# A fused transformer kernel on one core: the GELU up projection as three float32r products of split operands

## The reference, cut to what matters

```python
sa = _mha(x, x, None, sq_w, sq_b, ...)
x = _self_output(sa, x, so_w, so_b, so_g, so_be)          # project, residual, layer norm
inter = jax.nn.gelu(x @ fi_w + fi_b, approximate=False)   # 2048 x 256 by 256 x 1024
x = _self_output(inter, x, fo_w, fo_b, fo_g, fo_be)       # 2048 x 1024 by 1024 x 256
```

## Time and profile before

| | us |
|---|---|
| median of 3 runs (1096.51 to 1098.58) | 1096.81 |
| span of the profiled execution (first to last instruction) | 1094.8 |
| PE busy | 1019.2 (93%) |
| DVE busy | 782.0 (71%) |
| ACT busy | 607.7 (56%) |
| POOL busy | 331.8 (30%) |
| mean granted TensorE clock | 0.975 |

### The profile page before, as it was taken

The page is one execution under the profiler, slowest core; times in us unless marked ns, Lnnn a source line. Parts: engine busy times, 40 slices in busy tenths (PEclk is TensorE's granted clock), DMA queues, the critical chain, the costliest instruction groups (busy, mean ns, idle before and its releaser), DMA issues.

```text
span 1094.8 us, 20748 instructions
## 1 busy us (share of the span) xinstructions
PE 1019.2 (93%) x7648; PEld 601.0 (55%) x7648; DVE 782.0 (71%) x1337; ACT 607.7 (56%) x1191; POOL 331.8 (30%) x724
## 2 busy tenths in 40 slices
PE   5999989999999999999988898989898999999998
PEld 3675666433333333333344665648677676576865
DVE  4786577689999999999723747546536756887565
ACT  2665554478888888888853123131222456556543
POOL 3422111001010343344103334373366433530000
PEclk9999999889999999999998997999999999999999
DMA  7302221451221212212125100021344301100000
GB/s 213 70 16 88 87 68 66 144 188 44 75 71 48 70 49 69 79 45 70 47 67 191 34 15 10 20 77 44 101 155 132 100 31 49 44 25 1 16 18 26
DMA packets 97578, 75.67 MB, mean 69 GB/s; under 512 B 49806, under 2 KB 87483, under 8 KB 97223
## 3 DMA queue, kind: packets, MB, share of 16 engines
q1 hardware_dynamic: 94407, 65.95, 20.0%
q0 software_dynamic: 3072, 8.39, 2.4%
HBM read 42.94 MB, written 30.93 MB: 67 GB/s over the span
## 4 chain that ended last, share of the span: by engine, by line
PE 65%; DVE 10%; DMA 8%; issue 5%; POOL 4%; ACT 4%; SPq 3%; POOLq 0%; DVEq 0%; ACTq 0%
PE OUT L855 15%; PE TR L855 14%; PE OUT L1090 9%; PE TR L861 8%; PE TR L1079 7%; DMA head_q<-MT 7%; PE OUT L1079 3%; PE TR L931 3%; PE SCR L915 2%; POOL dispatched L2038 2%; SPq L697 2%; ACT PTS L1298 2%; PE SCR L908 2%; DVE small L1486 1%; PE OUT L861 1%
## 5 line engine op out<-in xcount | busy, mean ns | idle before, releaser
L1555 DVE TENSOR_REDUCE small<-SCR 128x1 f32<-128x1024 f32 x256 | 308.5, 1223 | 26.2 <-PE SCR L962 20.3
L1396 ACT ACTIVATE shared<-TR 128x512 f32<-128x512 f32 x352 | 200.1, 597 | 38.8 <-PE TR L1079 30.7
L962 PE MATMUL SCR<-head_k,head_q 48*128 48x512 f32 x512 | 193.9, 456 | 2.7 <-DVE P L1531 2.7
L1090 PE MATMUL OUT<-shared,HM 128*32 128x256 f32 x2048 | 165.3, 394 | 1.2 <-ACT shared L1396 0.4
L1079 PE MATMUL TR<-head_q,head_k 51*128 51x512 f32 x352 | 149.7, 463 | 0.9 <-issue 0.6
L1919 POOL TENSOR_SCALAR small<-small 128x1 f32<-128x1 f32 x112 | 27.7, 247 | 346.7 <-DVE small L1487 344.5
L855 PE MATMUL TR<-xT,fifo 128*128 128x512 f32 x224 | 105.8, 629 | 1.1 <-ACT xT L1276 1.0
L1396 ACT ACTIVATE shared<-OUT 128x512 f32<-128x512 f32 x160 | 95.8, 599 | 19.3 <-PE OUT L1079 17.6
L1079 PEld LDWEIGHTS TR<-head_q,head_k 51*128 51x128 f32 x352 | 60.6, 186 | 76.4 <-ACT shared L1396 56.5
L1276 ACT ACTIVATE xT<-TR 128x256 f32<-128x256 f32 x96 | 35.4, 381 | 111.5 <-PE TR L861 108.6
L1090 PEld LDWEIGHTS OUT<-shared,HM 128*32 128x32 f32 x2048 | 41.4, 108 | 93.1 <-ACT shared L1396 57.6
(11 more groups left out here) (241 smaller groups left out, 1860.3 us busy)
## 6 DMA issues: line engine op xcount, KB each, us to landing
pieces<-pieces SPq DMA_DIRECT2D x16, 512.0 KB, 2.7
HM<-dispatched SPq DMA_DIRECT2D x46, 128.0 KB
expert_out<-HM SPq DMA_DIRECT2D x46, 128.0 KB
dispatched<-HB SPq DMA_DIRECT2D x6, 768.0 KB, 4.0
head_q<-pieces SPq DMA_DIRECT2D x32, 128.0 KB
head_k<-pieces SPq DMA_DIRECT2D x32, 128.0 KB
shared<-in_L_ffn_w SPq DMA_DIRECT2D x4, 1024.0 KB, 12.0
x<-TOK SPq DMA_DIRECT2D x16, 128.0 KB, 1.7
```

Source lines behind the costliest of these rows:

```text
L962: ins = nc.tensor.matmul(SQ[kt % 2][:, hf, :], QX[n % 2][rows, kt * 128:(kt + 1) * 128], KX[n % 2][rows, hf * 512:(hf + 1) * 512], start=T ...
L1090: ins = nc.tensor.matmul(PV[32 * g:32 * g + 32, 0:256], VH[:, n % 2, kt, :], PTB[:, kt % 2, g * 256:(g + 1) * 256], start=(kt == 0), stop= ...
L1396: nc.scalar.activation(PTB[:, kt % 2, hf * 512:(hf + 1) * 512], ring_bank("t_scores", n, kt, hf), ACT.Exp, scale=DH ** -0.5).then_inc(st_d ...
L1555: nc.vector.tensor_reduce(nm[:, n % 2, kt:kt + 1], SQ[kt % 2].rearrange("p h n -> p (h n)"), AX, ALU.max, negate=True).then_inc(sq_done.se ...
```

## The change

`fi` is split in two float32r parts, high (`FIH`, in the place of `P`) and low (`FIL`, in the place of `fi` itself), by GpSimd in heads 1 to 8: a cast and a subtraction of 256 columns in each. The transposed input is split as well: `LX.t` now transposes into a bank of OUT, ScalarE copies the bank as float32r into `XGH`, and VectorE subtracts `XGH` from the bank into `XGL` and gives the bank back. `FI.k` has six float32r products for each m (high by high, high by low, low by high, for both halves of the features) instead of two float32 products. As `P` is used for the parts, its last columns are zeroed again by a new step `PZ` (one memset of VectorE) late in the experts. In the diff `gelu_input` stands three times, in TensorE's, ScalarE's and VectorE's stream in this order. The table of steps is otherwise unchanged.

```diff
-    "LX": dict(tr=1),
+    "LX": dict(out=1, xhi=1),
+    "PZ": dict(),
...
-HT.34 QP.0 DM.5 CG.7 RX.5 XL.37 DN.34 UP.36 YS.33 XL.38 S.0 XT.37 HT.35 XT.38 UP.37 XL.39 L3.5 HT.36 E.0 CB.4 UP.38
+HT.34 PZ QP.0 DM.5 CG.7 RX.5 XL.37 DN.34 UP.36 YS.33 XL.38 S.0 XT.37 HT.35 XT.38 UP.37 XL.39 L3.5 HT.36 E.0 CB.4 UP.38
...
+        FIH = over("gelu_up_high", [128, KD, F], F32R, "P")
+        FIL = over("gelu_up_low", [128, KD, F], F32R, "fifo")
+        XGH = over("gelu_in_high", [128, KD, N], F32R, "xT3")
+        XGL = over("gelu_in_low", [128, KD, N], F32R, "P", KD * F)
...
+                def gelu_input(t):
+                    pe.wait_ge(tok_ready.sem, tl.after(tok_ready, "SN", t))
+                    bank = out_bank(tl)
+                    transposes(bank, [XN[:, t % BT, k * 128:(k + 1) * 128] for k in range(KD)]).then_inc(out_full.sem, 1)
+
                 def gelu_up(k):
-                    at.block_copied("LX", k)
+                    pe.wait_ge(out_done.sem, tl.after_block(out_done, "LX", k))
+                    pe.wait_ge(fi_ready, 1)
                     for m in range(MF):
-                        at.feature_major(fi, xTb, m)
+                        c = slice(m * 128, (m + 1) * 128)
+                        bank = tr_bank(tl)
+                        product(bank, [(w[:, f, c], x[:, f, :]) for f in range(KD)
+                                       for w, x in ((FIH, XGH), (FIH, XGL), (FIL, XGH))]).then_inc(tr_full.sem, 1)
...
+                def gelu_input(t):
+                    bank = OUT[:, tl.slot(out_full, 2), :]
+                    act.wait_ge(out_full.sem, tl.next(out_full))
+                    c = t % BT * 128
+                    nc.scalar.activation(XGH[:, :, c:c + 128], bank[:, 0:256].rearrange("p (k n) -> p k n", k=KD), ACT.Copy)\
+                        .then_inc(xg_ready.sem, 1)
...
+                def gelu_input(t):
+
+                    bank = filled(tl)
+                    dve.wait_ge(xg_ready.sem, tl.next(xg_ready))
+                    c = t % BT * 128
+                    signal_out(tl, nc.vector.tensor_tensor(
+                        XGL[:, :, c:c + 128], bank[:, 0:256].rearrange("p (k n) -> p k n", k=KD),
+                        XGH[:, :, c:c + 128].bitcast(F32), ALU.subtract))
+
+                def key_columns():
+
+                    dve.wait_ge(tr_full.sem, tl.after(tr_full, "FI", T // BT - 1))
+                    nc.vector.memset(P[:, :, :, SC1:KP], 0.0)
...
             for n in range(NH):
+                if n == 1:
+                    pool.wait_ge(d_fifo, 16 * 2)
+                if 1 <= n < 1 + 4 * KD:
+                    k, c = divmod(n - 1, 4)
+                    part = (slice(None), k, slice(c * 256, (c + 1) * 256))
+                    chain(nc.gpsimd.tensor_copy(FIH[part], fi[part]))
+                    ins = nc.gpsimd.tensor_tensor(FIL[part], fi[part], FIH[part].bitcast(F32), ALU.subtract)
+                    if n == 4 * KD:
+                        ins.then_inc(fi_ready, 1)
...
-                pool.wait_ge(tr_done.sem, tl.after(tr_done, "LX", t))
+                pool.wait_ge(out_full.sem, tl.after(out_full, "LX", t))
                 add_bias(XN[:, t % BT, :], "fo_b")
```

More of the change, by code:

```diff
@@ L272, in schedule_c @@
             before((a, i - 2), (b, i))
+    before(("PZ",), ("S", 0))
     for k in range(T // BT):
+        before(("FI", k), ("PZ",))
         before(("FI", k), ("L3", 0))
@@ L566, in build @@
         placed = Signal(sem("slots_placed"), **count("place"))
+        xg_ready = Signal(sem("gelu_in_high_ready"), **count("xhi"))
         h_ready = Signal(sem("high_parts_ready"), **count("top"))
@@ L570, in build @@
                   "pc": (pc_ready,), "gate": (gate_exp,), "act": (a_ready,), "low": (l_ready,),
-                  "pick": (picked,), "place": (placed,)}
+                  "pick": (picked,), "place": (placed,), "xhi": (xg_ready,)}
         d_rb = [sem(f"residual_loaded_{r}") for r in range(BT)]
@@ L596, in build @@
         wscale_ready = sem("weight_scales_ready")
+        fi_ready = sem("gelu_weights_split")
         tern_ready = Signal(sem("ternary_ready"), b=(1 + KD) * MF)
@@ L1255, in _ @@
                     "ST": self_output_transposes, "SO": self_projection,
-                    "LX": lambda t: at.transposed(XN[:, t % BT, :], ("SN", t)),
+                    "LX": gelu_input,
                     "FI": gelu_up, "FO": gelu_down,
@@ L1445, in _ @@
                 tl.walk(order_c, groups, attention(tl, SC1, cols["bq"], xTs) | {
-                    "ST": lambda t: copy_transposed(tl, xTs, t), "LX": lambda t: copy_transposed(tl, xTb, t),
+                    "ST": lambda t: copy_transposed(tl, xTs, t), "LX": gelu_input,
                     "FI": gelu_up, "L2": lambda t: copy_transposed(tl, XTR[:, t % 2], 0), "GT": gates_exp,
@@ L1843, in _ @@
                 tl.walk(order_c, groups, attention(tl, chain, SC1) | {
-                    "VW": lambda b: pass_start(tl, KB1[:, b, :], VS1[0:KP, b, :, :]), "SN": self_norm, "FN": gelu_norm,
+                    "VW": lambda b: pass_start(tl, KB1[:, b, :], VS1[0:KP, b, :, :]), "SN": self_norm, "LX": gelu_input, "PZ": key_columns, "FN": gelu_norm,
                     "SO": lambda t: with_residual(tl, chain, t, XN[:, t % BT, :], RB[:, t % BT, :], "RS"),
@@ L1996, in _ @@
             tl = Tally("b")
-            chain = Chain(0, 3 * (NH - 2) + MF * (3 + 2 * KD))
+            chain = Chain(0, 3 * (NH - 2) + 4 * KD + MF * (3 + 2 * KD))
             for n in range(NH):
+                if n == 1:
[7 more added lines that the diff above has]
+                        ins.then_inc(fi_ready, 1)
                 i = n - (MF + KD + 3)
```

## The result

| | before | changed |
|---|---|---|
| median, runs side by side, us | 1096.66 (4 runs) | 1106.24 (4 runs, 1103.52 to 1113.48) |
| ratio, 95% interval | | 1.0098 [1.0054, 1.0141] |
| span of the profiled execution | 1094.8 | 1102.3 |
| granted clock in it | 0.975 | 0.964 |

Two later groups of runs gave 1.0087 [1.0058, 1.0115] and 1.0087 [1.0051, 1.0124]. The forecast was +2.0 us, its range ended at 1103.0.

What follows compares the result with a forecast made beforehand. TensorE was taken as the bound, with 65% of the chain. Terms: 2.0 + 5.9 + 1.5 - 3 x 2.75 + 0.1 + 0.7 = +2.0 us on a 1094.8 us span, plus 2.0 to the median: 1098.8 us, range 1094.5 to 1103.0.

Steps and rivals of the forecast that it cites:

- ahead of FI.0: Before block 0's up projection: VectorE's added subtractions and waits make it start 2.0 us later (1.6 to 2.4).
- gap to FI.1: Before block 1's up projection: its last subtraction queues behind two normalisation steps on VectorE, so it starts 5.9 us later.
- gap to FI.2: Before block 2's up projection: a router product's wait for a bank and the last subtraction add 1.5 us (1.0 to 2.2).
- gap to FI.3: Before block 3's up projection: the last transposes wait for a router copy behind a normalisation, so it starts 3.6 us later.
- four blocks shorter: Up projections: 48 float32r products 0.229 us apart take 11.0 us against 13.75, gaining 2.75 us a block.
- behind FI.3's end, up to the transfer: After block 3: its end comes 0.85 us later, TensorE's 0.76 us idle before the dispatched tile absorbs nearly all, leaving +0.1.
- clock, over all: Longer idling before blocks: 0.5 us more half speed in each of three blocks, half lost, +0.7 us (0 to +5).
- Rival A: In the up projections, products come at 0.215 us, gaining 10.2 us, time 1096.9 us; chance 0.21.
- Rival B: Ahead of the blocks, waits cost only the work, VectorE's block 1 backlog being off the path: 1093.5 to 1095.5 us; chance 0.12.

## Why the prediction was wrong

Each step against the mean of three profiles a side, in us:

| step | forecast | measured |
|---|---|---|
| ahead of FI.0 (from the last head) | +2.0 | +2.4 |
| gap to FI.1 | +5.9 | +6.2 |
| gap to FI.2 | +1.5 | +2.4 |
| gap to FI.3 | +3.6 | +4.3 |
| four blocks shorter | -11.0 | -9.7 (2.7, 2.7, 2.5, 1.8) |
| behind FI.3's end, up to the transfer | -0.75 (idle 0.76 absorbs) | +0.6 |
| clock, over all | +0.7 | in the rows above |
| sum | +2.0 | +6.2 |
| medians | +2.0 | +9.6 |

- **The mechanisms were right.** Products 0.231 us apart (0.229), subtractions of 0.41 to 0.44 us, blocks 0 to 2 of 12.8 to 13.2 us (13.1), FI.1 6.2 us further from FI.0's end with FN.2 and FN.3 (L1521, L1522, L1766, then the moments L1511 and L1512) straight ahead of its subtraction, no wait for the first dispatched tile, no cost of the weights' split in its median. Rival A is out: products do not come at 0.215 us. The Trainium skill, page "TensorE: Matmul & The Clock Gate", section "Wait — 56ns, not 53.3ns?", gives 215.7 ns at 512 columns for warm back-to-back matmuls; this case measured 231 for float32r, 15 above it. Rival B is out: taking the queue of FN.2 and FN.3 away gave back 4.0 us.
- **The steps that failed are sizes, above all in blocks 2 and 3.** The waits ahead of them were put at +1.5 and +3.6 us and measured +2.4 and +4.3. The gain of block 3 was booked at 2.75 us and is 1.8. And the idle 0.76 us in front of the dispatched tile did not absorb what it was booked for: the wait for the tile is gone, but 0.25 us for ScalarE stand in its place, and the first product of a later dispatched tile (`OUT<-shared,MW`) comes only 0.4 us nearer to block 3's end (16.1 us behind it; 16.5 in the mean of before). The rest of the way to the transfer varies by more than what is missing. Nearly all misses have one sign, and their sum, a good 4 us, is twice the forecast.
- **Clock was costed in the wrong place.** I put 0.7 us into longer half-speed stretches inside blocks 0 to 2. There they hardly grew. They grew in the gap ahead of block 3 (mean clock 0.99 before, 0.91 after: 25.87 x 0.01 x 2 = 0.5 us at half speed became 30.16 x 0.09 x 2 = 5.4) and in block 3 itself (15.18 x 0.09 x 2 = 2.7 became 13.60 x 0.18 x 2 = 4.9; all three profiles of the changed kernel have 0.82). Close to half of the added 2.2 us is lost, 1.0 us by estimate, and that is what block 3's gain lacks. In the gap, part of the half-speed time is idle and costs nothing. That it makes up the missed 0.7 us there is argued, not shown.
- **The range was too narrow for its reference.** The stretch accounts for 6 of the 9.6 us. The rest does not lie behind the transfer: from there to the last instruction it is 129.1 to 130.5 us in the three profiles of before and 129.1 to 130.6 in those of the changed kernel. It lies ahead of the last head, where profiles of before alone differ by 7.8 us, or in the 2 to 4 us by which the stretch itself scatters. Two of the three intervals (+5.4 to +15.5, +6.4 to +12.6, +5.6 to +13.6 us) hold the 6.2 us of the traces, and the second begins just above it. Whether the change has a share in the remaining 3.4 us stays open: the weights' split alone showed none in its median, yet the medians of the changed kernel came out high three times, and the first heads lean the same way.

## What to carry to other kernels

A faster operand path on the bound engine pays only if no other engine is put in series ahead of it: here 10 us of shorter products bought 15 us of waiting, 4 of them through two steps that stood in the queue of VectorE ahead of a 0.4 us instruction. When work is added to an in-order queue, the table of order has to be made anew around it, since steps that were free under the bound engine are not any more. And of a sum of many small waits, each counted from the shortest way through it, the errors add up with one sign: here 2.3 us over four gaps.

## What the hardware showed

- A float32r product of 128 rows and 512 columns takes 0.231 us at the full clock and 0.43 at half: half speed costs it a factor of 1.85, not 2. A float32 product has two instructions 0.43 us apart; three float32r products take 0.69 us in place of 0.86, a fifth less.
- With overwritten products in the idle stretch ahead of it, block 1 ran at 1.00 from its first instruction, in two kernels: 11.38 us in place of 13.01. Ahead of three other blocks such products did nothing: 13.5 to 13.6 us, at 0.82 to 0.83.
- Half speed can come with TensorE busy nearly throughout: busy 38.4 of 40 us in the heads, clock 0.66 in that stretch of one execution, with the same program at 1.00 in the others. The thirteen other profiles have 1.00 from 250 to 560 us. The last head of that execution lay 15.7 us later than in the second profile of the same kernel.
